# Moving the middle of a four-layer graph kernel to tile groups: the head of the MLP loop, the expert rows, the weight halves and the last source scatters

## The reference, cut to what matters

```python
x = x + gnn(layernorm(x), src, dst, edge_weight, ...)          # scatter-add over 50000 edges, then relu(h @ w1 + b1) @ w2 + b2
x = x + ffn(layernorm(x))                                      # routed to one of 8 experts, 489 rows each at most
#   y_tok = ybuf[idx, pos_g] * (prb * kept)[:, None]
#   y = nan_to_num(y_tok, nan=0.0, posinf=10000.0, neginf=-10000.0)
x = x + typed_gnn(layernorm(x), node_type, edge_index, ...)    # K, Q, V by type; softmax per destination and per source
#   h = concatenate([agg, agg], axis=1);  o = typed_linear(h, Wa, ba, node_type)
x = x + slice_attention(layernorm(x), ...)
```

## Time and profile before

| | us |
|---|---|
| median of 3 runs | 4656.86 (4652.67 to 4658.95) |
| profiled execution, its own time | 4656.4 |
| span of its trace | 4654.7 |
| PE busy, share of the span | 61% |
| DVE busy | 55% |
| POOL busy | 58% |
| ACT busy | 35% |

### The profile page before, as it was taken

One profiled execution on the slowest core, in us unless ns is written; L12 is line 12 of the kernel. 1 busy time (PEld: TensorE's weight loads), 2 busy tenths in 40 slices (PEclk: granted clock), 3 DMA queues, 4 the chain that ended last, 5 costly groups with the idle time before them and its releaser, 6 DMA issues.

```text
span 4654.7 us, 58284 instructions
## 1 busy us (share of the span) xinstructions
PE 2832.3 (61%) x13865; PEld 1900.4 (41%) x13967; DVE 2553.8 (55%) x5223; ACT 1626.7 (35%) x4287; POOL 2703.0 (58%) x2564
## 2 busy tenths in 40 slices
PE   3200015555548850378877698867877788583887
PEld 1000013334435430135544477744544677461334
DVE  7545445555320008148999755579999544425332
ACT  1111100000111110026666577756666677520220
POOL 3777777777677768557777344467776344430000
PEclk6555557777769975698999799989999899875997
DMA  8334357333434462788998655578888455330000
GB/s 335 137 141 150 136 124 249 105 105 105 97 134 157 153 204 65 148 247 269 275 275 273 159 141 143 140 214 274 271 271 245 101 140 140 98 109 15 0 0 28
DMA packets 763184, 741.87 MB, mean 159 GB/s; under 512 B 385177, under 2 KB 650482, under 8 KB 762948
## 3 DMA queue, kind: packets, MB, share of 16 engines
q1 hardware_dynamic: 640536, 395.13, 29.4%
q0 software_dynamic: 115760, 316.99, 23.0%
q10 hardware_dynamic: 6672, 27.26, 1.4%
HBM read 480.90 MB, written 267.14 MB: 161 GB/s over the span
## 4 chain that ended last, share of the span: by engine, by line
DVE 23%; PE 22%; issue 19%; POOL 10%; DVEq 6%; DMA 4%; SPq 2%; ACT 1%; POOLq 0%; ACTq 0%
DVE BIGR L1244 10%; POOL AR L1467 6%; PE ps L575 5%; DVE AR L1264 5%; DVEq L1260 4%; PE ps L870 3%; PE ps L879 3%; PE ps L1810 2%; POOL rec_src L462 2%; DVE BIGR L555 1%; DMA AR<-typ_x 1%; PE ps L1811 1%; PE ps L1960 1%; DMA BIGR<-in_L_ffn_w 1%; PE ps L1112 1%
## 5 line engine op out<-in xcount | busy, mean ns | idle before, releaser
L1220 POOL DMA_INDIRECT AR<-kv_tab,META x832 | 791.9, 952 | 271.5 <-issue 255.4
L1467 POOL TENSOR_TENSOR AR<-AR 128x896 f32<-128x896 f32 x208 | 351.4, 1689 | 525.0 <-ACT AR L1527 525.0
L437 POOL DMA_INDIRECT rec_dst<-AR,slot_e x400 | 441.0, 1103 | 185.3 <-issue 121.6
L1444 DVE TENSOR_TENSOR BIGR<-BIGR,ps 128x260 f32 x832 | 353.6, 425 | 307.6 <-PE ps L1500 157.2
L1244 DVE TENSOR_REDUCE BIGR<-ps 128x8 f32<-128x1024 f32 x416 | 507.6, 1221 | 17.9 <-PE ps L1353 2.9
L462 POOL DMA_INDIRECT rec_src<-AR,slot_e x400 | 420.7, 1052 | 125.0 <-issue 121.5
L1500 PE MATMUL ps<-AR 128*128 128x260 f32 x1664 | 427.0, 400 | 82.3 <-POOL AR L1467 73.0
L575 PE MATMUL ps<-AR 128*128 128x256 f32 x832 | 299.6, 524 | 290.0 <-issue 210.5
L529 POOL DMA_INDIRECT AR<-xn_tab,META x416 | 394.6, 948 | 132.5 <-issue 121.2
L1500 PEld LDWEIGHTS ps<-AR 128*128 128x128 f32 x1664 | 299.4, 192 | 173.0 <-DVE BIGR L1444 129.4
L575 PEld LDWEIGHTS ps<-AR 128*128 128x128 f32 x832 | 207.6, 261 | 382.8 <-issue 336.3
(11 more groups left out here) (395 smaller groups left out, 5932.4 us busy)
## 6 DMA issues: line engine op xcount, KB each, us to landing
v_dst<-AR SPq DMA_DIRECT2D x104, 384.0 KB, 4.3
AR<-v_dst SPq DMA_DIRECT2D x104, 384.0 KB, 3.5
v_src<-AR SPq DMA_DIRECT2D x104, 384.0 KB, 4.8
AR<-v_src SPq DMA_DIRECT2D x104, 384.0 KB, 3.4
AR<-in_W_qvk SPq DMA_DIRECT2D x44, 608.0 KB
rec_dst<-BIGR ACTq DMA_DIRECT2D x1, 26624.0 KB, 90.2
rec_raw<-AR SPq DMA_DIRECT2D x40, 640.0 KB, 3.0
AR<-rec_raw POOLq DMA_DIRECT2D x40, 640.0 KB, 4.4
```

The costliest lines, as they stand in the source:

```text
L437: pool.indirect_dma_start(rec_tab[0], bass.IndirectOffsetOnAxis(ap=slot_e[0][:, c * CC + k:c * CC + k + 1].bitcast(U32), axis=0), RD[s][0] ...
L1220: pool.indirect_dma_start(KVR[s][:, u, 0:KV], None, kv_tab, bass.IndirectOffsetOnAxis(ap=META[o][:, g * U + u, 0:1].bitcast(U32), axis=0)) ...
L1444: ve.tensor_tensor(a, a, PS[4 + u][:, 0:SROW], ALU.add).then_inc(sem("add"), 1)
L1467: pool.tensor_tensor(v, v, VB[s][:, :, D:SROW].unsqueeze(3).to_broadcast([P, U, H1, DK]), ALU.mult).then_inc(sem("pv"), 1)
```

## The change: what it does

- **MLP head.** A third buffer `HS` is added. DVE forms `h(0)` ahead of the loop and in each step `h(step+1)` ahead of the tail of `step-2`.
- **Experts.** SP's and DVE's programs are written out instead of looped. Both upper parts of `Wa` and the first lower piece are loaded behind the first two row loads; further lower pieces, three types each (seven in all), one after each expert's write. The space is that of `META[1]`. DVE, not POOL, adds a piece in experts 1 to 7.
- **Expert rows.** The 25 gathers form four groups (4, 7, 7, 7 tiles). ACT multiplies by the gate and normalizes, DVE replaces and adds in seven pieces of three or four tiles by other instructions (five passes where there were seven), and takes statistics and roots by group. `types_pool` waits by group.
- **Source scatters.** The chunks are split 7, 25, 3, and the last 5 chunks (50 scatters) go into POOL's first sum pass, one behind each of the first 50 `weigh` instructions. SP loads them on chip after chunk 34; it reads `META[1]` in the first sum pass behind groups 62, 70, 78 and 86. POOL's and SP's first sum pass is written out.

The diff, cut to its core:

```diff
+        CL = 35
+        R2T = [BIGR[:, NT * SROW + CC * REC * k:NT * SROW + CC * REC * (k + 1)] for k in range(NCK - CL)]
...
+        def src_tail_sync(sp):
+            for j in range(4):
+                sp.wait_ge(sem(f"r2_sent{j}"), 16 * CC * len(range(j, CL, 4)))
+            sp.wait_ge(sem("x2"), 1)
+            for c in range(CL, NCK):
+                sp.dma_start(R2T[c - CL], rec_raw[c * P:(c + 1) * P, :]).then_inc(sem("tail_in"), 16)
...
+            def head(t):
+                if t >= 3:
+                    ve.wait_ge(sem("mlp_ht"), t - 2)
+                ve.scalar_tensor_tensor(out=HS[t % 3], in0=XN[:, t, :], scalar=epsc, in1=ACC[:, t, 0:D],
...
+            head(0)
             for step in range(N2 + 2):
...
+                if step + 1 < N2:
+                    head(step + 1)
...
+            def low_half(j):
+                if j:
+                    sp.wait_ge(sem("wa_sum"), j)
+                t0, n = WAR[j]
+                for k in range(2):
+                    sp.dma_start(WLOW[:, 0:n, k * D:(k + 1) * D], wa[:, t0:t0 + n, 2 + k, :]).then_inc(sem("wa_in"), 16)
...
+            for i in range(EX // 2):
                 for s in range(2):
                     e = 2 * i + s
...
+                    if i:
+                        sp.wait_ge(sem("ex_y"), 4 * (e - 1))
+                    sp.dma_start(XE[s], xin[:, 4 * e:4 * e + 4, :]).then_inc(sem(f"ex_in{s}"), 16)
...
+                if i == 0:
+                    for k in range(2):
+                        sp.dma_start(WSR[:, :, k * D:(k + 1) * D], wa[:, :, k, :]).then_inc(sem("wa_in"), 16)
+                    low_half(0)
                 for s in range(2):
                     e = 2 * i + s
                     sp.wait_ge(sem("ex_ys"), 4 * (e + 1))
...
+                    sp.dma_start(yout[:, 4 * e:4 * e + 4, :], YB).then_inc(sem("ex_out"), 16)
+                    if 0 < e < len(WAR):
+                        low_half(e)
...
+                if e:
+                    ve.wait_ge(sem("ex_out"), 16 * e)
+                    t0, n = WAR[e - 1]
+                    ve.wait_ge(sem("wa_in"), 32 * (e + 1))
+                    ve.tensor_tensor(WSR[:, t0:t0 + n, :], WSR[:, t0:t0 + n, :], WLOW[:, 0:n, :], ALU.add).then_inc(sem("wa_sum"), 1)
...
+        XGRP = (0, 4, 11, 18, N2)
+        XSUB = ((0, 4), (4, 8), (8, 11), (11, 15), (15, 18), (18, 22), (22, N2))
+        BAD, REP = ar(0, 4 * D, dt=I32), ar(1024, 4 * D)
...
+            def normal(k):
+                act.wait_ge(sem("nmr"), k + 1)
+                for t in range(XGRP[k], XGRP[k + 1]):
+                    act.activation(XNI[:, t, 0:D], X[:, t, :], ACT.Identity, scale=rs[:, 3, t:t + 1], bias=nmr[:, t:t + 1]
+                                   ).then_inc(sem("xn"), 1)
+
+            def roots(k):
+                sl = slice(XGRP[k], XGRP[k + 1])
+                act.wait_ge(sem("var"), VAR3 + k + 1)
+                act.activation(rs[:, 1, sl], rs[:, 0, sl], ACT.Sqrt).then_inc(sem("sd"), 1)
+
+            for k in range(4):
+                act.wait_ge(sem(f"rows{k}"), 64 * (NG // SL) + 16 * (XGRP[k + 1] - XGRP[k]))
+                for t in range(XGRP[k], XGRP[k + 1]):
+                    act.activation(YG[:, t, :], YG[:, t, :], ACT.Identity, scale=gate_p[:, t:t + 1]).then_inc(sem("gated"), 1)
+                if k >= 2:
+                    roots(k - 2)
+                    normal(k - 2)
+            for k in range(2, 4):
+                roots(k)
+                normal(k)
+
...
+            def normal(k):
+                sl = slice(XGRP[k], XGRP[k + 1])
+                ve.wait_ge(sem("sd"), VAR3 + k + 1)
+                newton(ve, rs, sl)
+                ve.scalar_tensor_tensor(out=nmr[:, sl], in0=mv[:, sl, 0], scalar=-1.0, in1=rs[:, 3, sl], op0=ALU.mult, op1=ALU.mult
+                                        ).then_inc(sem("nmr"), 1)
+
+            due = None
+            for a, b in XSUB:
+                y = YG[:, a:b, :].rearrange("p t d -> p (t d)")
+                n = (b - a) * D
+                ve.wait_ge(sem("gated"), b)
+                ve.tensor_scalar(BAD[:, 0:n], y, 0.0, 0.0, ALU.mult, ALU.not_equal)
+                ve.tensor_scalar(REP[:, 0:n], y, FMAX, None, ALU.is_gt)
+                ve.drain()
+                ve.scalar_tensor_tensor(out=REP[:, 0:n], in0=y, scalar=-FMAX, in1=REP[:, 0:n], op0=ALU.is_lt, op1=ALU.subtract)
+                ve.drain()
+                ve.tensor_scalar(REP[:, 0:n], REP[:, 0:n], -10000.0, None, ALU.mult)
+                ve.drain()
+                ve.copy_predicated(y, BAD[:, 0:n], REP[:, 0:n])
+                ve.drain()
+                x = X[:, a:b, :].rearrange("p t d -> p (t d)")
+                ins = ve.tensor_tensor(x, x, y, ALU.add)
+                if b == N2:
+                    ins.then_inc(sem("x2"), 1)
+                ve.drain()
+                for t in range(a, b):
+                    ve.bn_stats(bst[:, t % 2, :], X[:, t, :])
+                    ve.drain()
+                    ve.bn_aggr(mv[:, t, :], bst[:, t % 2, :])
+                ve.drain()
+                if due is not None:
+                    normal(due)
+                    due = None
+                if b in XGRP:
+                    due = XGRP.index(b) - 1
+                    sl = slice(XGRP[due], b)
+                    ve.tensor_scalar(rs[:, 0, sl], mv[:, sl, 1], LN_EPS, None, ALU.add).then_inc(sem("var"), 1)
+            normal(due)
...
+        WAR = [(t, min(3, T1 - t)) for t in range(0, T1, 3)]
+        WLOW = META[1][:, :, :].rearrange("p b c -> p (b c)")[:, 0:3 * 2 * D].rearrange("p (t c) -> p t c", c=2 * D)
...
+            for k in range(4):
+                pool.wait_ge(sem("xn"), 2 * NT + XGRP[k + 1])
+                for t in range(XGRP[k], XGRP[k + 1]):
...
+            for g in range(NG):
+                load(g // SL, g % SL)
+                q = (g - META_AT) // 8
+                if g >= META_AT and (g - META_AT) % 8 == 0 and q < MP[1]:
+                    if q == 0:
+                        sp.wait_ge(sem("tail_sent"), 16 * CC * (NCK - CL))
+                    meta_piece(sp, 1, q)
+
+        META_AT = CC * (NCK - CL) + 12
...
+            pool.wait_ge(sem("tail_in"), 16 * (NCK - CL))
+            for g in range(NG):
+                weigh(g // SL, g % SL)
+                if g < CC * (NCK - CL):
+                    c, k = CL + g // CC, g % CC
...
+                        rec_tab[1], bass.IndirectOffsetOnAxis(ap=slot_e[1][:, c * CC + k:c * CC + k + 1].bitcast(U32), axis=0),
...
+                    ).then_inc(sem("tail_sent"), 16)
...
-            wa_sync(sp)
-            meta_sync(sp, 1)
+            src_tail_sync(sp)
...
-            scatter_src_pool(pool, 0, 10)
+            scatter_src_pool(pool, 0, 7)
             route_pool(pool)
-            scatter_src_pool(pool, 10, 34)
+            scatter_src_pool(pool, 7, 32)
             expert_rows_pool(pool)
-            wa_pool(pool)
-            scatter_src_pool(pool, 34, NCK)
+            scatter_src_pool(pool, 32, CL)
```

169 lines of the change are left out of this document (59 added, 110 removed).

## The result

The changed kernel takes 4510.86 us (median of 4 runs, 4503.27 to 4513.36) against 4656.37 for the kernel before in the same comparison (4652.67 to 4658.95): a ratio of 0.9684, with a 95% interval of 0.9673 to 0.9696. That is 146 us less than the 4657 shown ahead, where 127 was forecast. 4511 lies in the range of 4505 to 4562, but 18 us under the forecast of 4529 and outside the forecast's own range of 4517 to 4541.

What follows compares the result with a forecast made beforehand. The chain of waits through MLP, experts, expert rows to types and typed projection was taken as the bound; -37 + 8 - 102 + 4 = -127 from 4656.4 gives 4529, range 4505 to 4562, own range 4517 to 4541.

Steps and rivals of the forecast that it cites:

- MLP, -37: MLP loop: ordinary step falls from 4.07 to 2.6 us; worked-out gain 39, taken as 37, bounds 20 and 43.
- Experts, +8: Experts' weight loads: `Wa` transfers in front delay three turns by 2.3 to 4 us each; 8 us taken.
- POOL's margin, 12 us: Experts' end: POOL finishes its 25 chunks at 1674, 12 us ahead of the experts' last write at 1686.
- Expert rows to types, 114: First gather to first typed rows: POOL's chain of 106 us plus 8 lost to DVE's passes, against 214 before.
- rival 2: Expert rows to types: DVE's passes hold POOL to their end, costing 33 us instead of 8; 4554 us, chance 0.14.
- The rule that I set against the earlier trace: Expert rows to types: only `tensor_scalar` passes would hold POOL, some 13 of 36 us, for a loss of 3 us.
- First sum pass, +4: First sum pass: 50 scatters cost nothing, at most 15 us; four `META` pieces cost 1 us each.
- Rival 5: Whole change: all covers hold, nothing lost for DVE's passes, experts' turns and `META`; 4509 us, chance 0.07.
- Rival 1: MLP: bound by the round through ACT, step 3.3 us; gain 20, time 4546 us, chance 0.15.
- rival 3: Queues: 12 us at the experts' turns and 8 us for each `META` piece; 4562 us, chance 0.11.
- rival 4: First sum pass: DVE's additions hold scatters; gain gone from 4.4 us each, 4797 us at 6.89; chance 0.03.

Runs made afterwards that it cites:

- 1: Kernel before with only the MLP head a tile ahead in three HS buffers: 5467.21 against 5499.94 us, ratio 0.9938.
- experiment 5: Changed kernel with its MLP head edit alone taken back: 5335.01 us against 5467.83 for the kernel before, ratio 0.9747.
- 6: Changed kernel with loads of expert e + 2 right behind the write of expert e: 5253.99 us against 5467.83 for the kernel before, ratio 0.9608.
- 7: Changed kernel with the three chunks between gathers and types moved into the first sum pass: 5291.52 us against 5467.83 for the kernel before, ratio 0.9671.
- 3: Changed kernel without the 50 scatters in its first sum pass: that pass took 376.4 us, with a period of 3.650; no total time given.
- experiment 11: Changed kernel with expert loads behind each write and chunks split 7, 23, 2, 8: 4464.76 us against 4654.68 for the kernel before, ratio 0.9591.
- experiment 4: Changed kernel without DVE's 35 instructions replacing non-finite values: first gather to first typed rows took 116.0 us; no total time given.
- experiment 10: Changed kernel run again unaltered on the chip of the last two runs: 4505.40 us against 4654.68 for the kernel before, ratio 0.9683.
- 2: Kernel before with SP's and POOL's loop of the first sum pass written out: 5500.61 against 5499.94 us, ratio 0.9993.
- 9: Changed kernel with 16 and 8 empty DVE instructions ahead of the sum passes' loops: 5296.84 us against 5463.14 for the kernel before, one run.
- 8: Changed kernel with early expert loads, 22 chunks beside experts, two in the middle, nine in the sum pass: 5221.51 us, ratio 0.9546 to the kernel before.
- experiment 12: Changed kernel without the 25 source chunks (250 scatters) beside the experts: 4682 us, one run; the experts took 335.5 us.

## Why the prediction was right, and where its sizes were off

**Which step bounds each stage** was read rightly: DVE's place in the MLP's loop (shown by 1 and 5), the pairs at the experts (6), POOL's chain in the middle (7), and POOL's slack in the sum pass (3). The 2.7 us of the typed projection fit the weights that have landed ahead of the rows, but no run tries this alone. The sizes were less good: all six stages came out better than forecast, by 23 us in all, and 7 us of it went in the rest of the span, for which nothing was forecast.

**MLP, -37, measured -42.7.** The ordinary step is 2.59 us (2.6 forecast), the idleness at a group's end 2.41 (2.7). From the first transposes to the last addition it is 1198.95 to 1280.01, 81.1 us, where my working had 84: to the first group's break 19.8 (20.7), three groups 50.8 (50), the last steps 10.5 (13). PE's idleness was less than forecast and the step behind it more (4.25, so 1.7 over an ordinary one, where 1 was allowed). So the mis-sized terms are the last five steps, which I counted at a full 2.6 each, and the 2 us that I took off the worked-out 39 without a row for it; 1 us more is in the routing (56.4 to 55.4).

**Experts, +8, measured +6.8.** The three waits grew from 44.0 to 50.5 us, 2.2 each, just under my 2.3 to 4. On the slower chips they were 36.0 without the lower pieces of `Wa` in front and 42.5 with them, again 2.2 each.

**POOL's margin, 12 us, measured 6.7 and 8.4.** The experts' last write was 5 us sooner than forecast, at 1680.8. POOL's last chunk ended at 1674.0, as worked out, but by luck: the slots came at 1302.54, 3.5 us sooner than my 1306, and from there POOL took 371.5 us where I had 368. The term that I put at nothing is what DVE's seven additions do to POOL. Six of them each held a scatter, 5.7 us in all; without that POOL would have been early by about 12. Experiment 11 shows that this margin is the next bound.

**Expert rows to types, 114, measured 110.5.** The passes' hold on POOL was sized at 8 us and is 5.0 (experiment 4, to POOL's first scatter by type); with the additions to `X`, which stayed in that run, it is 6.8. The count of instructions and their 1.25 to 1.28 us hold. For rival 2 the account is mixed. Its mechanism, DVE's passes hold POOL to their end, is what the trace shows, and also what the earlier trace rows had shown: the scatter of 1.91 us at 306.26 ended 0.84 us behind the DVE pass beside which it started, so these rows were not against it. Its price of 33 us is wrong, since it took 26 whole scatters as lost. What a hold costs is what is left of the pass when the transfer starts, less 0.1 us, and these passes are only 0.6 to 1.3 us long.

The rule that I set against the earlier trace rows, of the Trainium skill (SBUF — State Buffer, "Who interferes with whom"), gave 3 us, since by it the `tensor_scalar` passes alone would hold POOL. Its inference, that the writing of descriptors is not held by a DVE instruction with two SBUF inputs, does not agree with this trace: a gather took 1.67 us beside L997 and a scatter 2.28 beside L934, both passes with two such inputs.

DVE was later than forecast, 77.6 in place of 70. It began at 8.3 (9 forecast) and then waited 1.77 us for ACT's gates and 5.45 for a root of ACT. This cost nothing: POOL needs the last seven tiles only 18 scatters after it comes to the types, at 1781.

**First sum pass, +4, measured -6.** This is the one term with the wrong sign. Its parts were right or high: a scatter 0.04 us where 0 was taken and 0.3 the bound, `META[1]` nothing where 1 us a piece was taken. What was missing is that the pass runs at another steady period, 3.650 in place of 3.707: 3 us over the 54 groups without scatters, and under 1 over the 34 with scatters behind the first 16. 2 to 3 us more lie in the first 16 groups (57.9 against 60.4), which vary as much from run to run of one kernel (57.9 and 60.5 in experiment 10, where the pass was 378.1, 3 us less than before). The period is not from SP's or POOL's loop (2), nor from scatters (3), nor from DVE's offset (9); what of the change sets it stays open.

**Rivals.** Rival 5, all covers hold, gave 4509; the time is 4511, but not by its road: the turns and DVE's passes do cost 6.8 and 5, and the MLP and the sum pass made up for them. Rival 1 is out by the step of 2.59 where it has 3.3, rival 3 by turns of 2.2 us each and by `META[1]` at no cost, rival 4 by scatters of 1.00 us in the sum pass. For rival 4 I also left the issue out of a sum: by its own terms the gain would be gone from a scatter of 4.1 us, not 4.4.

## What to carry to other kernels

Write the margins of whatever runs beside a stage down with the sum, for the smallest of them is the next bound: here 6.7 to 8.4 us, so that of the 54 us of waits that experiment 11 took away 34 came back, most of them because two chunks of 13.4 us were moved out of POOL's way as well. Work that is moved to an engine with idle time can still slow its neighbour: ask what that neighbour starts beside it (here DVE's additions took 5.7 us from POOL's margin). Work of a queue with idle time in each period of a later pass is nearly free there, at 0.04 us for a scatter of 1.27 with its issue, as long as the loads of the pass are not set back: a transfer of 8 us every 18 cost nothing, every 11 it cost 15 us. Loads of the next weights belong behind the write that frees their buffer, not behind the pair.

## What the runs showed of the hardware

**A transfer that POOL starts beside a DVE pass can be held to the pass's end.** An indirect transfer of 0.97 us that starts while one of the passes named next runs ends 0.8 to 0.9 us behind it. In the changed kernel: behind L934 (`tensor_tensor`, 1536 columns, six transfers) 0.84 to 0.85, behind L997 (`scalar_tensor_tensor`, five) 0.84 to 0.90, behind L1001 (`copy_predicated`, five) 0.79 to 0.83, behind L999 (`tensor_scalar`, two) 0.84 to 0.86. In the kernel before it was 0.85 behind a pass of 7.09 us and 0.83 behind one of 7.51. All of these have their operands in on-chip memory alone. Other passes held nothing: beside L1306, a `tensor_tensor` with one input from the accumulator memory, 160 transfers took 0.94 to 0.96 us, with up to 1.04 us of the pass left; beside L1313, a `tensor_reduce` in on-chip memory, 154 took 0.94 to 0.95.

**A loop over five engines has several steady periods.** The same sum pass, in its groups without a scatter, settled at 3.650, 3.707, 3.727 or 3.753 us a group, each level kept within 0.01 us over the pass and the same in run after run. The second pass has 3.753 in the kernel before and in all of the twelve but experiment 4. There it has 3.727, and the first pass 3.707; the only difference from the changed kernel is 35 DVE instructions some 950 us ahead of the first pass.

**Issue can stall with nothing to wait for.** On the slower chips PE started its products in the first experts only every 2.80 us. Experiment 5:

```profile
1651.07 0.59 PE L898 MATMUL ps<-BIGR 128*128 128x256 f32 x1 [2.21 <-issue]
1653.87 0.59 PE L898 MATMUL ps<-BIGR 128*128 128x256 f32 x1 [2.21 <-issue]
```

They waited for nothing that the profile shows, and the experts took 637 us, where 346 are needed on the other chip. In experiment 5 such gaps make 188 us at the experts, one of them alone 84, and all lie where POOL scatters. The last chunk of scatters ended at 1874.9 us, and between 1850 and 1900 PE was back to 30.8 busy us of 50, from 9.3 between 1700 and 1750. With 22 chunks beside the experts in place of 25 they took 552 us in place of 582 (8 against 6). DVE's 1.40 us in experiment 4 is half of PE's 2.80, and the first of those instructions fell beside scatters.

Against scatters as the cause stand two rows. The last two DVE instructions shown in experiment 4 came 1.40 us apart, at 2232.03 and 2233.43, while POOL had no scatter under way (from 2230.3 to 2240.9). And in experiment 5, on a slower chip too, DVE's same instructions came 0.25 us apart beside the same scatters. So the cause stays open; experiment 12 was meant for it and ran on the other kind of chip.
